# State-space layer: read-out states summed by accumulating transposes, time on partitions, turned back once a group

## The reference, cut to what matters

```
h_n[t] = exp(dt[t] * A_n) * h_n[t-1] + dt[t] * x[t] * B_n[t]     for n in 0..15
y[t]   = sum over n of h_n[t] * C_n[t]  +  D * x[t]               summed over both directions
out    = (y * silu(z)) @ W_out.T
```

## Time and profile before

| | us |
|---|---|
| median of 3 runs | 4592.76 (4589.97 to 4595.15) |
| the profiled execution | 4601.28, span 4599.5 |
| PE busy, share of the span | 4145.6, 90% |
| DVE busy | 3250.3, 71% |
| POOL busy | 3215.3, 70% |
| ACT busy | 2413.6, 52% |
| mean granted TensorE clock | 0.949 of full speed |

### The profile page before, as it was taken

The page is one execution under the profiler, slowest core; times in us unless marked ns, Lnnn a source line. Parts: engine busy times, 40 slices in busy tenths (PEclk is TensorE's granted clock), DMA queues, the critical chain, the costliest instruction groups (busy, mean ns, idle before and its releaser), DMA issues. The chain is left out here.

```text
span 4599.5 us, 63372 instructions
## 1 busy us (share of the span) xinstructions
PE 4145.6 (90%) x17184; PEld 2234.8 (49%) x17184; DVE 3250.3 (71%) x5016; ACT 2413.6 (52%) x4880; POOL 3215.3 (70%) x1671
## 2 busy tenths in 40 slices
PE   7988958996999999999999999999999974999994
PEld 5666646672344344344334434433433434666773
DVE  5777762121899999999899999999989986112124
ACT  3566632223766766666676666667667544222221
POOL 3233213441999999999999999999999971444441
PEclk7999987997999999999999999999999987999997
DMA  1000023451343333433333333333333321344466
GB/s 34 25 21 23 15 64 87 122 151 52 108 119 116 120 112 112 124 112 120 120 115 112 112 115 121 113 115 116 122 112 115 111 85 49 109 117 118 134 185 227
DMA packets 264754, 478.66 MB, mean 104 GB/s; under 512 B 37044, under 2 KB 174084, under 8 KB 264548
## 3 DMA queue, kind: packets, MB, share of 16 engines
q1 hardware_dynamic: 235776, 403.02, 27.8%
q0 software_dynamic: 28032, 73.17, 6.4%
q10 hardware_dynamic: 740, 0.49, 0.0%
HBM read 409.60 MB, written 41.81 MB: 98 GB/s over the span
## 5 line engine op out<-in xcount | busy, mean ns | idle before, releaser
L1818 POOL TENSOR_TENSOR m_xh<-m_u,m_Bb 128x1536 f32<-128x1536 f32 x512 | 1776.9, 3539 | 58.1 <-DVE m_u L1689 44.9
L1745 PE MATMUL bank<-m_xh,ident 128*128 128x512 f32 x3072 | 1459.7, 611 | 36.3 <-POOL m_xh L1807 36.3
L1787 DVE TENSOR_TENSOR_SCAN bank<-bank,m_xh 128x512 f32<-128x512 f32 x864 | 1039.0, 1216 | 45.1 <-ACT bank L1774 41.9
L1774 ACT ACTIVATE bank<-m_dt,m_Ac 128x508 f32<-128x508 f32 x1536 | 1024.7, 683 | 38.4 <-DVE m_xh L1787 38.4
L1745 PEld LDWEIGHTS bank<-m_xh,ident 128*128 128x128 f32 x3072 | 577.2, 194 | 828.6 <-issue 737.1
L1787 DVE TENSOR_TENSOR_SCAN m_xh<-bank,m_xh 128x512 f32<-128x512 f32 x672 | 787.7, 1207 | 71.5 <-ACT bank L1774 66.0
L1807 POOL TENSOR_TENSOR m_xh<-m_xh,m_Cb 128x1536 f32<-128x1536 f32 x224 | 791.2, 3532 | 4.8 <-DVE m_xh L1787 4.5
L1798 DVE TENSOR_TENSOR m_xh<-bank,m_Cb 128x512 f32<-128x512 f32 x864 | 580.8, 672 | 9.8 <-DMA m_Cb<-BC_rows 9.8
L1204 ACT ACTIVATE f1t_h<-bank,f1t_b 128x512 f32<-128x512 f32 (+1 forms) x276 | 142.8, 589 | 471.3 <-PE bank L1239 471.3
L1593 PE MATMUL bank<-m_xp,m_dg 128*128 128x512 f32 x768 | 352.4, 601 | 3.7 <-DVE m_u L1689 1.4
L1134 POOL DMA_INDIRECT rows_y<-f1t_y,f1t_home x142 | 140.3, 988 | 272.7 <-DVE f1t_y L1175 243.4
(11 more groups left out here) (367 smaller groups left out, 6002.0 us busy)
## 6 DMA issues: line engine op xcount, KB each, us to landing
m_Bb<-BC_rows SPq DMA_DIRECT2D x256, 512.0 KB, 4.9
m_Cb<-BC_rows SPq DMA_DIRECT2D x256, 512.0 KB, 4.1
f1t_w<-f_w SPq DMA_DIRECT2D x46, 576.0 KB
m_r<-m_dt POOLq DMA_DIRECT2D x32, 768.0 KB, 7.4
f1t_w1a<-f_w SPq DMA_DIRECT2D x46, 384.0 KB
f0t_w<-f_w SPq DMA_DIRECT2D x22, 576.0 KB
f1c_yg<-rows_y SPq DMA_DIRECT2D x16, 768.0 KB, 8.3
f1t_w1b<-f_w SPq DMA_DIRECT2D x92, 96.0 KB
```

The lines of the kernel that those rows point to most:

```text
L1745: mm = pe.matmul(bank[:, c, :], K.ident[:, :], xh[n % NX][:, c, :], start=False, stop=(d == 1 and n == NS - 1))
L1774: act.activation(o[:, :, lo:hi], seqs(dt[d][:, c, :])[:, :, lo:hi], ACT.Exp, scale=Ac[:, c, n:n + 1]).then_inc(s_dA, 1)
L1787: dve.tensor_tensor_scan(o, bank[:, RING[d][p], way], xh[n % NX][:, c, way], 0.0, ALU.mult, ALU.add).then_inc(s_h, 1)
L1818: pool.tensor_tensor(xh[n % NX][:, :, :], u[d][:, :, :], Bb[q % RB][:, n % QN, :].unsqueeze(1).to_broadcast([P, DC, TOK]), ALU.mult).then_ ...
```

## The change

The sums of a group are no longer made by a matmul with the identity as weights and 512 moving columns. Now each 128-column block (one sequence j) of the product is the weights, the identity moves through, and the instruction is a transpose that accumulates. The sums then stand with time on partitions, 12 blocks in banks 0 to 2 (`place`). The D term becomes four matmuls of 128 columns for each chunk, in the same layout. At the end of a group ACT copies the three banks to SBUF (`act_yt`, slots 6, 6, 7, waiting for all sums of the group), PE transposes the 12 blocks back (`pe_yT`, slots 4, 5, 5), and `dve_y` waits for that. Slots move too: `dve_y` to 6, 7, 8, `pe_D0` to 9, 10, 11, where each now waits for all three `dve_y`; and the nine late sums go three to a slot into slots 0, 1, 2.

```diff
-            "y": (6, 7, 9), "pe_D0": (14, 15, 17), ...
+            "act_yt": (6, 6, 7), "pe_yT": (4, 5, 5), "y": (6, 7, 8), "pe_D0": (9, 10, 11), ...
...
+        yt = dt[1]
+        def place(j, c):
+            return divmod(j * DC + c, G)
+        def sums(j, c):
+            b, k = place(j, c)
+            return bank[:, b, k * P:(k + 1) * P]
...
         def pe_D(pe, g, d, c):
             pe.wait_ge(s_xc, g * 2 + d + 1)
             if d == 0 and later(g):
-                pe.wait_ge(s_gy, (g - 1) * DC + c + 1)
+                pe.wait_ge(s_gy, g * DC)
...
-            pe.matmul(bank[:, c, :], dgD[:, c, :], xc[d][:, c, :], start=(d == 0), stop=False).then_inc(s_D, 1)
+            for j in range(G):
+                b, k = place(j, c)
+                opens = d == 0 and c == 0 and (j == 0 or b != place(j - 1, c)[0])
+                mm = pe.matmul(sums(j, c), xc[d][:, c, j * P:(j + 1) * P], dgD[:, c, :], start=opens, stop=False, skip_group_check=True)
+            mm.then_inc(s_D, 1)
...
         def pe_sum(pe, g, d, n, c):
...
-            mm = pe.matmul(bank[:, c, :], K.ident[:, :], xh[n % NX][:, c, :], start=False, stop=(d == 1 and n == NS - 1))
+            for j in range(G):
+                closes = d == 1 and n == NS - 1 and c == DC - 1 and (j == G - 1 or place(j, c)[0] != place(j + 1, c)[0])
+                mm = pe.matmul(sums(j, c), xh[n % NX][:, c, j * P:(j + 1) * P], K.ident[:, :], start=False, stop=closes,
+                               is_transpose=True, skip_group_check=True)
             mm.then_inc(s_red, 1)
+
+        def act_yt(act, g, b):
+            act.wait_ge(s_red, (g + 1) * 2 * UNITS)
+            act.copy(yt[:, b, :], bank[:, b, :]).then_inc(s_yt, 1)
+
+        def pe_yT(pe, g, c):
+            pe.wait_ge(s_yt, (g + 1) * DC)
+            for j in range(G):
+                b, k = place(j, c)
+                mm = pe.transpose(bank[:, c, j * P:(j + 1) * P], yt[:, b, k * P:(k + 1) * P], K.ident[:, :])
+            mm.then_inc(s_yT, 1)
...
         def dve_y(dve, g, c):
-            dve.wait_ge(s_red, (g * 2 * NS + 2 * NS - 1) * DC + c + 1)
+            dve.wait_ge(s_yT, g * DC + c + 1)
...
         def sums_at(carry):
...
-                begun = sum(p >= at for at in POS["pe_D0"])
-                if carry and begun < DC:
-                    upto = min(upto, begun)
-                now = list(range(done, min(upto, done + 2)))
+                if carry:
+                    begun = sum(p >= at for at in POS["pe_D0"])
+                    upto = min(3 * (p + 1) - LAG * DC, 0) if begun < DC else upto
+                now = list(range(done, min(upto, done + 3)))
...
                 def main(pe, g, d, p, end):
                     carry = d == 0 and later(g)
+                    if carry:
+                        for c, at in enumerate(POS["pe_yT"]):
+                            if at == p:
+                                pe_yT(pe, g - 1, c)
...
                 def main(act, g, d, p, end):
                     act_decay(act, g, d, p)
+                    if d == 0 and later(g):
+                        for b, at in enumerate(POS["act_yt"]):
+                            if at == p:
+                                act_yt(act, g - 1, b)
```

More of the change, by code:

```diff
@@ L1381, in mamba_phase @@
         POS = {
-            "y": (6, 7, 9), "pe_D0": (14, 15, 17), "pe_D1": (6, 16, 25), "pe_out": (17, 18), "out": (14, 15),
+            "act_yt": (6, 6, 7), "pe_yT": (4, 5, 5), "y": (6, 7, 8), "pe_D0": (9, 10, 11), "pe_D1": (6, 16, 25), "pe_out": (17, 18), "out": (14, 15),
             "act_rows": (11, 13), "rows": (12, 14), "stats": 14, "rstd": 18, "norm": 40,
@@ L1449, in mamba_phase @@
         s_gy, s_ops, s_out = sem("gated_ready"), sem("outps_ready"), sem("res_ready")
+        s_yt, s_yT = sem("sums_copied"), sem("sums_turned")
+        yt = dt[1]
[4 more added lines that the diff above has]
+            return bank[:, b, k * P:(k + 1) * P]
         def seqs(t):
@@ L1930, in after @@
                             pe_sum(pe, NG - 1, 1, n, c)
+                    for c in range(DC):
+                        pe_yT(pe, NG - 1, c)
                     for i in two:
@@ L1938, in main, with after @@
                     act_decay(act, g, d, p)
-                program(act, "act", main, lambda act: None, lambda act: None)
+                    if d == 0 and later(g):
+                        for b, at in enumerate(POS["act_yt"]):
+                            if at == p:
+                                act_yt(act, g - 1, b)
+                def after(act):
+                    for b in range(DC):
+                        act_yt(act, NG - 1, b)
+                program(act, "act", main, lambda act: None, after)
             @block.gpsimd
```

## The result

The changed kernel takes 4711.0 us (median of four runs, 4705.9 to 4719.5) against 4591.7 for the kernel before in the same session: ratio 1.026, 95% interval 1.024 to 1.028. It is slower by 119 us, where +80 was forecast (4673, range 4588 to 4732). The profiled execution took 4711.2, of which the span is 4709.4.

The account below looks back on a forecast made before the run. POOL was taken to bound the kernel: its idle time grows from 3.2 to 8.5 us a group, +5.3 at fifteen boundaries, +80 on the 4592.8 median, 4673 us. Range 4588 to 4732; the first two cases alone 4630 to 4690.

Parts of the forecast that it names:

- The ceiling of 48 us: Most a lighter PE could gain: POOL's 3.2 us of waits a period, times 15 boundaries, 1.0%.
- the chain: At the boundary: third gating, D0 and D1, projection, `act_pj`, decay 11, scan 11, then POOL's read of step 3, 8.3 us late.
- both falls of the clock: PE idles some 5 us before T and about 4.6 before D0; half clock expected at both, chance 0.38, 4673 us.
- T: Moment at the boundary when POOL's read of step 14 ends; POOL wants to read step 3 at T+20.4.
- the other waits: POOL's waits besides the read of step 3: 1.0 us for PE's sums to vanish, 1.9 for `u` to become 0.2.
- The sum: Forecast total for a group: POOL's idle time from 3.2 us to 8.3 + 0.2 = 8.5, so +5.3.
- the first two cases: Half clock before T and before D0 (4673, chance 0.38), or only at the second place (4638, chance 0.22).
- the rival "slower still": Transposes leave PE's clock low, so convolution 1 and softplus sums come later: 9.1 us a group, 4730, chance 0.12.
- its other form: D term's passes at their upper bound: D0 and D1 3.4 us longer at half clock, 51 us over forecast, 4724.
- 5.3 a boundary: Forecast growth of POOL's idle time at each of fifteen boundaries, in us; +80 us in all.

Follow-up runs that it names:

- the sums as matmuls: Changed kernel with the sums as plain matmuls by the identity into the same places, without the transposing mode: 4921.0 us, ratio 1.071.
- the best kernel: Changed kernel with d = 1 projection ahead of D0 and D1, boundary fillings, zero passes at PE's other waits, and seven more pairs of these: 4560.2 us, ratio 0.9923.
- the run with transposes: Changed kernel with the first d = 1 convolution made twice before T and 32 transposes as filling ahead of D0: 4650.0 us, ratio 1.013.
- the order alone: Changed kernel with only the projection of d = 1 put ahead of D0 and D1 in PE's queue: 4742.2 us, ratio 1.030.
- the clock alone: Changed kernel with the projection left behind D0 and D1, filling passes at the boundary and zero passes at PE's other waits: 4645.0 us, ratio 1.009.
- the two together: Changed kernel with the projection first, fillings at the boundary and zero passes ahead of PE's other waits: 4575.9 us, ratio 0.9954.
- the run with order and clock together: Changed kernel with the projection first, eight filling passes before T and six ahead of the projection: 4639.3 us, ratio 1.009.

## Why the prediction was right, and where it was off

**Right: what bounds the kernel.** POOL sets the period. In every run the period was POOL's own 160.0 to 160.5 us and its waits for scans, sums and `u`, within 1 us (after: 160.4 + 9.7, measured 170.7; the sums as matmuls: 160.4 + 24.5, measured 185.4 in the mean). Busy and idle time add up for any engine; that the bound is POOL shows where the waits are gone: the period is 160.5 then, nearly all of it POOL's work, while PE is busy 91% of the time and DVE 93%. The ceiling of 48 us held: the best kernel gained 36.

**Right: the chain, and both falls of the clock.** The convolution ended at T+7.4 (7.7 forecast), the third gating at T+17.9 (18.75), D0 and D1 took 3.38 us (3.4), the projection ended at T+24.4 (26.0), and POOL's read waited 6.7 us (8.3). The places were shown one by one: holding the clock before T takes 2.3 us off that wait at most boundaries (2.4 forecast), at both places 3.9, which leaves 2.8 (3.2 forecast). The projection ended 1.6 us early, half because the third gating came early and half because the level rose in it: 3.01 us for 3.8.

**Off: the other waits.** The sum let POOL's waits for PE's sums vanish and those for `u` shrink to 0.2, on the ground that PE is freed. Measured, in one period, they are 1.9 and 0.8 (1.0 and 1.9 before). That is 2.5 us more than forecast against 1.6 less for the read: 9.6 in place of 8.5 us of idle time, 0.2 of it at another read. The step that failed is "What it can bring is the 1.0 us that POOL waits for PE": a freed PE has more idle places, and its clock falls at more than the two that I looked at: in the steps for dt, ahead of softplus sums, at the projection of d = 0. Holding it up there took these waits away (4639 to 4576 to 4560).

**How near the number was.** 4711 lies in the range, but outside the 4630 to 4690 of the first two cases, and nearer to the 4724 and 4730 of the rival "slower still" than to 4673. That the miss was no larger is partly luck: the read's wait was forecast too long and the other waits too short, and the two errors took something off each other. That rival had a longer wait for `u` from half clock late in the half; measured, the wait for `u` shrank to 0.8. Its cause, transposes that leave the clock low, is excluded at D0 by the run with transposes; its other form, D passes twice as long, by the 3.38 us that D0 and D1 took at half clock. Whether the short transposes have a part in the falls elsewhere is open.

**Where the 119 us are.** By the starts of POOL's L97, which runs once a group, 13 periods grew from 163.4 to 170.7 us (94 us), the first from 160.8 to 174.3 (13.5; part of it was an early start), and the stretch from the last to the next phase, with the fifteenth boundary and the openly standing copies, from 297.4 to 304.2 (7); the first of them came 4.7 earlier. That makes 110, the difference of the two spans (4709.4 and 4599.5); the other 9 are that the kernel before was profiled in one of its longer executions. Against the forecast's 5.3 a boundary, the 13 periods have 25 us more, 7.2 each: 1.5 of the 1.9 are POOL's waits, the rest its own work. The two ends have 5 more, and with the 9 that makes the 39.

**Order or clock: both, and they don't add.** From 4711, the order alone gives nothing (+31 by the medians, not clear of noise), the clock alone -66 (all over, 4645), the two together -135 (4576). With a low clock an earlier projection only puts something else late; with a late projection a high clock leaves POOL waiting.

## What to carry to other kernels

Work taken off an engine that isn't the bound gave nothing here by itself, and on TensorE it cost: its idle times grew, the granted clock fell from 0.98 to 0.87, and short bursts behind a wait took twice as long just where others wait for them. When instructions are reordered, follow what the one that is moved back holds up on every other engine; here one projection behind a wait was worth 109 us with none of the change's own work, some 90 of them (fifteen times 6.0) by the order alone. Passes that add zeros, put in front of PE's waits, are a cheap test of whether the clock is the cause, and were here the cure as well.

## What the hardware showed that I had not expected

- The granted clock fell without a long idle time, and how long PE idled did not tell whether it would. Before the change 2.95 us of idling left the level alone, while 2.94 us ahead of the early projection did not. In the old layout with the projection late, the same 1.98 us ahead of the third D term, behind the same work, were followed by a fall at eight boundaries and by none at seven. After the change the level fell around gaps of 1.1 us and less in the steps for dt, and after 2.2 to 2.4 us ahead of a projection and a softplus sum. What decides it no run settles; transposes back to back did hold the level.
- A stretch at half clock can last: 13.7 us in the steps for dt after the change (1687.9 to 1701.6), with PE busy 13.0 of them.
- A D pass of 128 columns took 0.21 us at half clock (16 in 3.38) and about 0.12 at full clock (24 in 2.94, in the run with order and clock together). The eight loads of D2 took 0.97 us after the change, 0.12 each, so load and columns do overlap.
